# First batch's x in four pieces with waits piece by piece, and four products of zeros on TensorE while it comes

## The reference, cut to what matters

```python
q = to_heads(hidden_states @ Wq, DK)
k = to_heads(hidden_states @ Wk, DK)
v = to_heads(hidden_states @ Wv, DV)
s = jnp.clip(to_heads(hidden_states @ Ws, M), CLAMP_MIN, CLAMP_MAX)
o = jnp.transpose(_chunk_abc(q, k, v, s), (0, 2, 1, 3))
g = (hidden_states @ Wg).reshape(b, t, H, DV)
...
x = _layernorm(x + _L0_attn_ref(...))
x = _layernorm(x + _L0_xattn_ref(x, ctx_1024, ...))
x = _layernorm(x + _L0_ffn_ref(x, ...))
```

## Time and profile before

| what | value |
|---|---|
| median of three runs | 1571.05 us (1569.86 to 1573.0) |
| the profiled execution's own time | 1571.14 us |
| its span, first to last instruction | 1569.2 us |
| mean granted TensorE clock | 0.993 |
| TensorE busy | 1520.3 us, 97% |
| VectorE busy | 1043.4 us, 66% |
| ScalarE busy | 652.4 us, 42% |
| GpSimd busy | 433.7 us, 28% |

### The profile page before, as it was taken

The page is one execution under the profiler, slowest core; times in us unless marked ns, Lnnn a source line. Parts: engine busy times, 40 slices in busy tenths (PEclk is TensorE's granted clock), DMA queues, the critical chain, the costliest instruction groups (busy, mean ns, idle before and its releaser), DMA issues.

```text
span 1569.2 us, 24173 instructions
## 1 busy us (share of the span) xinstructions
PE 1520.3 (97%) x9570; PEld 1203.8 (77%) x9570; DVE 1043.4 (66%) x1988; ACT 652.4 (42%) x1245; POOL 433.7 (28%) x282
## 2 busy tenths in 40 slices
PE   6999999999999999999999999999999799999996
PEld 5888888888888888888788888877878656666664
DVE  4556665565556666655666577686787976787786
ACT  4333333333323333333434334324333355867664
POOL 1111011110214344434454323221331234333310
PEclk9999999999999999999999999999999989999999
DMA  7112111120202122222232201101210413544551
GB/s 261 63 37 75 44 48 55 54 68 28 74 1 88 58 78 67 75 68 68 81 101 88 81 28 48 61 8 34 61 55 12 150 47 108 155 128 143 154 175 61
DMA packets 107552, 121.17 MB, mean 77 GB/s; under 512 B 5296, under 2 KB 75056, under 8 KB 107312
## 3 DMA queue, kind: packets, MB, share of 16 engines
q1 hardware_dynamic: 103984, 113.33, 23.0%
q10 hardware_dynamic: 3456, 6.29, 1.1%
HBM read 92.34 MB, written 27.26 MB: 76 GB/s over the span
## 4 chain that ended last, share of the span: by engine, by line
PE 85%; DVE 7%; issue 3%; DMA 2%; ACT 1%; POOL 1%; SPq 0%; POOLq 0%; DVEq 0%; ACTq 0%
PE bank L438 18%; PE bank L440 16%; PE bank L439 16%; PE bank L649 6%; PE bank L547 3%; PE bank L664 3%; PE bank L685 3%; PE bank L483 2%; PE bank L533 2%; PE bank L509 2%; PE bank L555 2%; PE bank L492 2%; PE bank L497 2%; PE bank L504 1%; PE bank L541 1%
## 5 line engine op out<-in xcount | busy, mean ns | idle before, releaser
L438 PE MATMUL bank<-Wh,X 128*128 128x512 f32 x512 | 211.0, 412 | 1.1 <-DVE Y L1086 1.1
L440 PE MATMUL bank<-Wh,X 128*128 128x512 f32 x512 | 200.8, 392 | 0.0
L439 PE MATMUL bank<-Wl,X 128*128 128x512 f32 x512 | 200.0, 391 | 0.0
L776 ACT ACTIVATE V<-bank 128x256 f32<-128x256 f32 x128 | 49.2, 384 | 324.1 <-PE bank L440 324.1
L438 PE MATMUL bank<-X,Wh 128*128 128x512 f32 x384 | 161.2, 420 | 12.3 <-DVE X L957 12.3
L1344 POOL TENSOR_TENSOR sm<-sm,half 128x8 f32<-128x8 f32 x32 | 52.8, 1650 | 396.5 <-DVE sm L1062 396.4
L1326 POOL TENSOR_TENSOR Wl<-RAW,Wh 128x512 fp32r<-128x512 f32 (+1 forms) x65 | 112.8, 1744 | 143.5 <-ACT Wh L731 143.5
L440 PE MATMUL bank<-X,Wl 128*128 128x512 f32 x384 | 151.3, 394 | 0.0
L439 PE MATMUL bank<-X,Wh 128*128 128x512 f32 x384 | 150.0, 391 | 0.0
L649 PE MATMUL bank<-XT,W 128*128 128x512 bf16 x512 | 123.5, 386 | 2.2 <-DVE M L1215 2.0
L1367 POOL TENSOR_TENSOR LO<-M,HI 128x512 fp32r<-128x512 f32 x64 | 82.0, 1281 | 152.1 <-PE bank L658 127.7
(11 more groups left out here) (190 smaller groups left out, 3252.5 us busy)
## 6 DMA issues: line engine op xcount, KB each, us to landing
z_scratch<-EV SPq DMA_DIRECT2D x64, 256.0 KB, 2.3
Z<-z_scratch SPq DMA_DIRECT2D x16, 1024.0 KB, 6.0
RAW<-wgT SPq DMA_DIRECT2D x16, 512.0 KB, 3.8
RAW<-wuT SPq DMA_DIRECT2D x16, 512.0 KB, 3.9
RAW<-wdT SPq DMA_DIRECT2D x16, 512.0 KB, 3.6
RAW<-Wo SPq DMA_DIRECT2D x14, 512.0 KB, 3.7
RAW<-Wv SPq DMA_DIRECT2D x26, 256.0 KB, 2.9
RAW<-Wg SPq DMA_DIRECT2D x26, 256.0 KB, 3.2
```

Of the source, the lines that this page charges most:

```text
L438: engine.matmul(o, lh(c), rh(c), start=c == 0, stop=False)
L439: engine.matmul(o, lh(c), rl(c), start=False, stop=False)
L440: last = engine.matmul(o, ll(c), rh(c), start=False, stop=c == n - 1)
L776: engine.activation(V[:, par, i, :], bk[:, 0:256], ACT.Copy).then_inc(S["v_evac"], 1)
```

## The change

The load of batch 0's x is cut into four pieces of one chunk each (256 KB), the first of which goes ahead of everything, also of Wq. The constants and small vectors are issued after the value and gate weights instead of first, and the loads of Y after those of x of batches 2 and 3. For step 0, TensorE waits chunk by chunk, and pass by pass, for the high part and the low part that the next product needs. Before that it makes four plain float32 products of 384 columns out of HK, which holds zeros, into a bank that nothing reads. VectorE no longer waits for the constants at its start. `load_x 2` moves into step 0, behind `states`, and `load_x 3` behind `weights`. The two semaphores of the last norm's moments become one, and AM and OG get a semaphore for each half.

```diff
@@ -47,13 +47,13 @@
 STEP = ("keys", "q", "scores", "states", "load_x", "tern", "k", "ok", "s", "turn_ok", "turn_o", "vg0", "tern",
-        "turn_w", "vg1", "y", "weights", "vg2", "values", "tern", "vg3")
+        "turn_w", "vg1", "y", "weights", "load_x", "vg2", "values", "tern", "vg3")
 OF_NEXT = ("q", "k", "s", "vg0", "vg1", "vg2", "vg3")
 def step_order(n, tasks):
-    terns = 0
+    terns = loads = 0
     for stage in STEP:
         m = n + 1 if stage in OF_NEXT else n - 1 if stage in ("turn_o", "y") else n
         if stage == "tern":
@@ -63,8 +63,9 @@
                     yield stage, t
                 del tasks[:1]
         elif stage == "load_x":
+            loads += 1
             if n == 0:
-                yield stage, 3
+                yield stage, loads + 1
         elif 0 <= m < STEPS:
             yield stage, m
@@ -101,7 +102,6 @@
     for stage in OF_NEXT:
         yield stage, 0
-    yield "load_x", 2
     tasks = list(range(52))
     for n in range(STEPS - 1):
         for stage, m in step_order(n, tasks):
@@ -210,7 +210,7 @@
 SEMAPHORES = """
-const_in vec_in raw0_in raw1_in am_in og_in v_in u_in y_in0 y_in1 y_in2 y_in3 ctx_in xw_in w3_in0 w3_in1 w3_in2 w3_store out_done
+const_in vec_in raw0_in raw1_in am0_in am1_in og0_in og1_in v_in u_in y_in0 y_in1 y_in2 y_in3 ctx_in xw_in w3_in0 w3_in1 w3_in2 w3_store out_done
 vec_made hk_zero
 x_hi x_lo_v x_lo_g w_hi w_lo_v w_lo_g wo_scaled w3_abs w3_sum w3_total w3_mean w3_round w3_clip w3_made
 proj_q proj_k proj_s proj_vg q_evac k_evac s_clip e_exp v_evac g_tanh u_made
@@ -343,24 +343,28 @@
         flat = lambda a: a.rearrange("p h i t -> p (h i t)")
-        raw = {0: RAW[:, 0, :], 1: RAW[:, 1, :], "am": flat(AM[:]), "og": flat(OG[:]),
+        raw = {0: RAW[:, 0, :], 1: RAW[:, 1, :], "am": flat(AM[:]), "og": flat(OG[:]), "am0": flat(AM[:, 0:1]),
+               "am1": flat(AM[:, 1:2]), "og0": flat(OG[:, 0:1]), "og1": flat(OG[:, 1:2]),
                "v": V[:, 1].rearrange("p i v -> p (i v)"), "u": U[:, 1].rearrange("p i v -> p (i v)")}
-        raw_in = {0: S["raw0_in"], 1: S["raw1_in"], "am": S["am_in"], "og": S["og_in"], "v": S["v_in"], "u": S["u_in"]}
+        raw_in = {0: S["raw0_in"], 1: S["raw1_in"], "am": S["am0_in"], "og": S["og0_in"],
+                  "am0": S["am0_in"], "am1": S["am1_in"], "og0": S["og0_in"], "og1": S["og1_in"], "v": S["v_in"], "u": S["u_in"]}
         x_raw = xT.rearrange("(c p) t -> p c t", p=128)
         wd = {k: w.rearrange("(c p) n -> p c n", p=128) for k, w in
               {"Q": Wq, "K": Wk, "S": Ws, "V": Wv, "G": Wg}.items()}
         wsrc = [w.rearrange("(c p) n -> p c n", p=128) for w in (wgT, wuT, wdT)]
-        first = [("Q", 0, 0), ("x", 0, 0, "am"), ("x", 0, 1, "og"), ("K", 0, 1), ("S", 0, 0), ("VG", 0, 0, "v"),
-                 ("VG", 0, 1, "u"), ("x", 1, 0, "am"), ("x", 1, 1, "og"), ("WO", 0, 0),
+
+        first = [("x", 0, 0, "am0"), ("Q", 0, 0), ("x", 0, 1, "am1"), ("x", 0, 2, "og0"), ("x", 0, 3, "og1"), ("K", 0, 1),
+                 ("S", 0, 0), ("VG", 0, 0, "v"), ("VG", 0, 1, "u"), ("x", 1, 0, "am"), ("x", 1, 1, "og"), ("WO", 0, 0),
                  ("x", 2, 0, 1), ("x", 2, 1, 0), ("x", 3, 0, 1), ("x", 3, 1, 0)]
         pieces = [(p[:-1], p[-1], 0) for p in first]
         pieces += [(key, i % 2, n) for i, (n, key) in enumerate(raw_tasks())]
         slot, landed, landings = {}, {}, {}
         for key, where, _ in pieces:
-            landings[where] = landings.get(where, 0) + (32 if key[0] == "VG" else 16)
-            slot[key], landed[key] = where, landings[where]
+            n = raw_in[where].name
+            landings[n] = landings.get(n, 0) + (32 if key[0] == "VG" else 16)
+            slot[key], landed[key] = where, landings[n]
         weight_no = {key: i + 1 for i, key in enumerate(key for key, _, _ in pieces if key[0] not in "xF")}
@@ -368,7 +372,7 @@
         def left_raw(key):
             if key[0] == "x":
-                return (S["x_lo_v"], 2 * key[1] + key[2] + 1) if key[1] < 2 else (S["x_lo_g"], 2 * key[1] + key[2] - 3)
+                return (S["x_lo_v"], 4 * key[1] + key[2] + 1) if key[1] < 2 else (S["x_lo_g"], 2 * key[1] + key[2] - 3)
             if key[0] == "F":
                 _, turn, k, j = key
                 return (S["w3_made"], 8 * k + j + 1) if turn else (S["w3_abs"], 8 * k + j + 1)
@@ -399,9 +403,15 @@
             else:
                 eng.wait_ge(S["proj_" + kind.lower()], n)
+        def x_columns(b, hc):
+            return slice(2 * hc, 2 * hc + 2) if b else slice(hc, hc + 1)
+
         def x_parts(b, hc):
-            cs = slice(2 * hc, 2 * hc + 2)
-            return raw[slot["x", b, hc]].rearrange("p (c t) -> p c t", c=2), X[:, b, 0, cs, :], X[:, b, 1, cs, :]
+            cs = x_columns(b, hc)
+            return raw[slot["x", b, hc]].rearrange("p (c t) -> p c t", t=T), X[:, b, 0, cs, :], X[:, b, 1, cs, :]
+
+        def x_high_count(b, hc):
+            return 2 * b + hc + 3 if b else hc + 1
         def ternary_of(t):
@@ -432,11 +442,19 @@
                 free[i] = freed
                 return banks[i]
-            def passes(o, lh, ll, rh, rl, n):
+            def passes(o, lh, ll, rh, rl, n, made=None):
+
                 for c in range(n):
+                    if made:
+                        for count in made(c)[0]:
+                            pe.wait_ge(*count)
                     engine.matmul(o, lh(c), rh(c), start=c == 0, stop=False)
+                    if made:
+                        pe.wait_ge(*made(c)[1])
                     engine.matmul(o, lh(c), rl(c), start=False, stop=False)
+                    if made:
+                        pe.wait_ge(*made(c)[2])
                     last = engine.matmul(o, ll(c), rh(c), start=False, stop=c == n - 1)
                 return last
@@ -444,18 +462,29 @@
                 b = PAIRS[n][1]
                 o = WOFF[kind]
                 bk = take((kind.lower(), n), freed)
-                pe.wait_ge(*left_raw(("x", b, 1)))
-                weight_ready(pe, kind, n)
+                made = None
+                if n == 0:
+
+                    made = lambda c: (((S["w_hi"], weight_no[kind, 0]), (S["x_hi"], c + 1)), left_raw(("x", 0, c)),
+                                      left_raw((kind, 0)))
+                else:
+                    pe.wait_ge(*left_raw(("x", b, 1 if b else 3)))
+                    weight_ready(pe, kind, n)
                 passes(bk[:], lambda c: Wh[:, c, o:o + 128], lambda c: Wl[:, c, o:o + 128],
-                       lambda c: X[:, b, 0, c, :], lambda c: X[:, b, 1, c, :], 4).then_inc(S["proj_" + kind.lower()], 1)
+                       lambda c: X[:, b, 0, c, :], lambda c: X[:, b, 1, c, :], 4, made).then_inc(S["proj_" + kind.lower()], 1)
             def project_vg(n, i):
                 b = PAIRS[n][1]
                 tl = slice(128 * i, 128 * i + 128)
                 bk = take(("vg", n, i), (S["v_evac"], 4 * n + i + 1), (S["u_made"], 4 * n + i + 1))
-                weight_ready(pe, "VG", n)
+                made = None
+                if n == 0:
+                    made = lambda c: (((S["w_hi"], weight_no["VG", 0, c // 2]),), left_raw(("VG", 0, c // 2)),
+                                      left_raw(("x", 0, c)))
+                else:
+                    weight_ready(pe, "VG", n)
                 passes(bk[:], lambda c: X[:, b, 0, c, tl], lambda c: X[:, b, 1, c, tl],
-                       lambda c: Wh[:, c, 384:896], lambda c: Wl[:, c, 384:896], 4).then_inc(S["proj_vg"], 1)
+                       lambda c: Wh[:, c, 384:896], lambda c: Wl[:, c, 384:896], 4, made).then_inc(S["proj_vg"], 1)
             def attend(stage, n):
                 par = n % 2
@@ -697,6 +726,11 @@
                 else:
                     attend(stage, n)
+
+            pe.wait_ge(S["hk_zero"], 1)
+            bk = take(("none",))
+            for i in range(4):
+                engine.matmul(bk[:, 0:384], HK[:, 0, :], HK[:].rearrange("p i n -> p (i n)"), start=True, stop=True)
             for stage, n in attention_order():
                 if stage in CROSS:
                     cross(stage, n)
@@ -913,13 +947,13 @@
                     engine.activation(HT[:, 0:8, :], bank("hq", i, 0)[:].bitcast(BF).rearrange("p (c t) -> p c t", c=8),
                                       ACT.Copy).then_inc(S["hq_evac0"], 1)
-            for p in first[:10]:
+            for p in first[:12]:
                 if p[0] == "x":
                     x_high(p[1], p[2])
                 else:
                     w_high(p[:-1])
-            act.wait_ge(S["x_lo_v"], 4)
+            act.wait_ge(S["x_lo_v"], 6)
             act.wait_ge(S["w_lo_v"], 5)
             act.wait_ge(S["const_in"], 16)
             engine.activation(IDB[:], IDN, ACT.Copy).then_inc(S["idb_made"], 1)
@@ -953,7 +987,7 @@
             def x_low(b, hc):
                 r, hi, lo = x_parts(b, hc)
-                dve.wait_ge(S["x_hi"], 2 * b + hc + 1)
+                dve.wait_ge(S["x_hi"], x_high_count(b, hc))
```

(40 more changed lines are left out.)

## The result

The changed kernel takes 1564.77 us (median of 12 runs, 1561.3 to 1567.49), against 1570.51 for the kernel before in the same measurements (12 runs, 1565.85 to 1574.92): a ratio of 0.996, 95% interval 0.9948 to 0.9972, or 5.7 us less. The prediction was 1565.0. The profiled execution took 1566.54 us, with a span of 1563.6; 2.9 us lie around the span here, 1.9 before.

What follows compares the result with a forecast made beforehand. TensorE, busy 97% of the span, bounds the kernel, its start delayed 12.3 us by a wait for x. Saving 6.3 us at the values less 0.2 for waits takes 1571.1 to 1565.0 us; range 1563.1 to 1568.0.

Steps and rivals of the forecast that it cites:

- The loads bound the row: Start of step 0: arriving loads limit TensorE's products; x's last piece at 8.1 us, Wk at 9.3, K's third product near 10.7.
- Zeros hidden: Start: zeros hold Q's first product by 0 to 1.1 us, made up because Q waits for its last piece at 9.4.
- Zeros worth nothing: Start: the zeros are credited with no gain, since Q's products would raise the clock mostly under cover of the loads.
- Values at 15.7, 6.3 us saved: Step 0: the values' first product begins at 15.7 us instead of 22.0, saving 6.3 us.
- VectorE late next, with 1 us of cover: Step 0: VectorE's chain about 1 us earlier, second gate product at about 30.2 us; TensorE wants its bank at some 31.3.
- Sum of 6.1 us: Whole kernel: 6.3 us saved at the values less 0.2 for waits gives 6.1 us.
- charge of 0.2 for waits: Step 0: some 16 more piece-by-piece waits on TensorE cost 0.2 us, bounds 0 and 1.
- `load_x` and Y at nothing: Later loads: moving `load_x 2` earlier, and Y behind x of batch 3, makes nobody wait.
- rival 1: Between Q and K: the clock falls, eight products cost 0.2 us more each; gain 4.5 us, 1566.6; chance 0.10.
- The pieces landed one behind the other: Start loads, against rival 2: four transfers share the engines, all landing at about 8.3 us; gain 4.8, 1566.3; chance 0.04.
- The fixed cost did not add up: Start loads, against rival 3: each transfer costs its 2.4 us alone, Wk at 14.1; gain 1.3 us, 1569.8; chance 0.08.
- stuck at `load_x 3`: Step 0, rival 4: ScalarE waits there for x of batch 3; at 57.2 us, 3.1 us slower, 1574.2; chance 0.04.

Runs made afterwards that it cites:

- old_places: Changed kernel with Y's loads ahead of x of batches 2 and 3, and their splits on ScalarE where they were before; 1571.91 us (one run).
- after_again: The changed kernel, unaltered, measured once more; 1564.82 us.
- no_zeros: Changed kernel without the four products of zeros, their bank still taken; 1563.34 us.
- const_late: Changed kernel with the constants and three small vectors issued behind Wo instead of ahead of batch 1's x; 1565.21 us.
- gates_first: Changed kernel with VectorE's sum and reciprocal of step 0 behind the four gate products instead of ahead of the second; 1562.3 us, ratio 0.9938 to the kernel before.
- The third profile: Profile of the changed kernel, unaltered, measured a third time; 1563.57 us.
- two_halves: Changed kernel with batch 0's x in two halves of 512 KB, the first ahead of Wq, and waits by halves; 1567.61 us (one run).
- whole_waits: Changed kernel with step 0's projections waiting for all of x and all of their weight; 1567.14 us (one run).

## Why the prediction was right, and where not

- **The loads bound the row: wrong.** The prediction had x's last piece at 8.1 and Wk at 9.3, and made K's third product wait for Wk's low part at 10.7. x's last piece landed by 7.0 and Wk at 7.7, just above the earliest, 7.0, that it allowed. The rate of 252 GB/s came from the kernel before; the new order reached 297. K then waited for nothing: once the zeros and Q's first pieces were through, TensorE's own 36 products set the time. With Wk at 7.7 the prediction's own working would have given a gain of 7.7 us, which is too much.
- **Zeros hidden: right in most executions, with the wrong piece.** They held Q's start, from 5.6 to 6.7, and the prediction had Q's later wait make that up, at its last piece. It was made up, at the second (old_places beside after_again), but for some 0.4 us in the profile of the kernel after. **Zeros worth nothing: wrong at the values**, by 1.0 to 1.5 us (no_zeros), because nine products would have been slow instead of none to two; at the root and in the time nothing of it can be told.
- **Values at 15.7, 6.3 us saved:** measured 15.1, 6.9 us, and 14.6 to 14.8 in others. Two errors stand against each other here: the loads were faster than charged, and TensorE's row then was the limit instead of them. That 15.1 came so near 15.7 is partly luck.
- **VectorE late next, with 1 us of cover: right place, wrong size.** Its chain came 0.1 us earlier instead of 1, because x of batch 1 was copied at 16.94, later than the 16.44 of before: it was issued at 10.84 (10.89 before), behind the constants. Issuing it earlier does not help, as Wo's scaling then waits for the small vectors (const_late). The wait cost 0.7 to 1.2 us; gates_first shows it was the reciprocal's place in VectorE's queue. The prediction had named both signs: "no new wait in PE before 50 us" did not hold, and the gate product held PE at 31 us, which it had listed as a sign of being wrong.
- **Sum of 6.1 us:** 6.2 at the root of step 0, 5.7 between the medians. The charge of 0.2 for waits and the missing 0.7 stand against 0.6 more at the values: the total is nearer than its terms, by luck. The third profile, 5.2 at the root, shows how far a single one can lie from it.
- **`load_x` and Y at nothing:** right for the change as it is, but the move is not idle. Without it the gain is gone (old_places, 6.9 us at the root).
- **The rivals.** No fall of the clock before K in the changed kernel, where Q's products never start more than 0.43 us apart once the zeros are through; but it fell in two_halves and in whole_waits, so rival 1 was one piece size away. The pieces landed one behind the other. The fixed cost did not add up: Wk landed earlier with two more pieces ahead of it, and four transfers of 256 KB beat two of 512 by 2.8 us at the values (half of it the clock) and 2.1 at the root. The Trainium skill ("DMA: Bandwidth & Descriptors", measured bandwidth) advises the larger transfers; the trace doesn't bear it out here, where the first consumer waits for the first piece. The fixed cost of about 2 us that the prediction names stands in another section of that page, on the anatomy of one DMA. ScalarE was not stuck at `load_x 3`: it copied at 47.7 without a wait. Not tested apart from the rest: Wq behind the first piece of x, the extra bank, and the merged semaphores.

## What to carry to other kernels

When TensorE bounds the kernel and a start-up load delays it, half of the delay was won here (6.2 of 12.3 us at the end of the first step), by two means: what is not needed leaves the front of the queue, and the first consumer waits for pieces. Giving TensorE something to do meanwhile brought a microsecond at the values and nothing behind VectorE's wait. After each, ask who was hidden by the late start: here two queues, ScalarE before a copy (5 us) and VectorE before a long reciprocal (0.7 to 1.2 us), came into view only then. Read such changes from a mark early in the trace, and take it from more than one execution; the total scattered by 6 us with the clock.

## What the runs showed that I had not expected

The move from the 1.2 to the 2.4 GHz level came 2.7 us after the first product in the kernel before, 4.0 in no_zeros, 2.8 after the gap in whole_waits, and only after some 6 us of zeros in the profile of the kernel after (products at 6.91 and 7.33 are 0.42 apart, at 7.33 and 7.56 0.23). Its moment varied between executions in which TensorE does the same until then: the four zeros took 5.49, 5.39 and 5.09 us in three of the changed kernel itself, and 4.27 to 4.77 in five variants.

After the 5.0 us wait in old_places and the 2.84 of whole_waits the level was low, as after the gaps of 1.12 and 0.24 us in two_halves. Such a wait cost more than its own length: some 2.6, 1.2 and 1.4 us on top in these three. The waits of 0.7 to 1.2 us for the gate product in the changed kernel did not: the products behind them start 0.23 us apart.
